# Attention kernel: the general path asked for behind each engine's own part, and more key tiles added on GpSimd in the last unit

## What is computed

```python
def _L0_gnn_ref(x, mask, Wq, bq, Wk, bk, Wv, bv, Wo, bo):   # 16 heads of 32
    q = heads(x @ Wq + bq); k = heads(x @ Wk + bk); v = heads(x @ Wv + bv)
    scores = jnp.einsum('bhqd,bhkd->bhqk', q, k) * scale
    scores = jnp.where(mask[:, None] == 0, -jnp.inf, scores)
    attn = jax.nn.softmax(scores, axis=-1)
    out = jnp.einsum('bhqk,bhkd->bhqd', attn, v)
    out = out.transpose(0, 2, 1, 3).reshape(b, s, D_MODEL)
    return out @ Wo + bo
h = jnp.maximum(_layernorm(x, axis=-1), 0.0)
x = x + _L0_gnn_ref(h, adj, Wq, bq, Wk, bk, Wv, bv, Wo, bo)
```

## Time and profile before

| | before |
|---|---|
| median of 3 runs (lowest to highest) | 1936.64 us (1936.35 to 1942.9) |
| the profiled execution, its own time | 1935.79 us |
| its span | 1933.9 us |
| mean granted clock of TensorE | 0.996 |
| PE busy | 1854.5 us (96%) |
| DVE busy | 1534.0 us (79%) |
| ACT busy | 1473.5 us (76%) |
| POOL busy | 1588.5 us (82%) |

### The profile page before, as it was taken

How to read it: one execution, slowest core, us unless ns; L and a number is a source line. 1 busy time by engine, 2 the same in 40 slices (tenths; PEclk the granted TensorE clock), 3 DMA queues, 4 the chain that set the end, 5 groups by cost and what they waited for, 6 DMA issues and landing times.

```text
span 1933.9 us, 35135 instructions
## 1 busy us (share of the span) xinstructions
PE 1854.5 (96%) x13856; PEld 767.9 (40%) x13856; DVE 1534.0 (79%) x1585; ACT 1473.5 (76%) x1772; POOL 1588.5 (82%) x701
## 2 busy tenths in 40 slices
PE   6989999999999999999999999999999999999997
PEld 4334434444344443444433443334344344343432
DVE  6788877887778887788877887778877788777775
ACT  4878886788867988678876788768887688867763
POOL 0988888887987979878889788888889889898873
PEclk9999999999999999999999999999999999999999
DMA  7532363523615335143442335423444224443121
GB/s 236 141 79 75 97 155 88 138 69 98 167 55 142 88 107 156 50 126 93 134 123 75 101 109 133 117 86 88 113 128 131 82 77 120 137 115 97 35 55 45
DMA packets 114136, 206.09 MB, mean 107 GB/s; under 512 B 12848, under 2 KB 16048, under 8 KB 113968
## 3 DMA queue, kind: packets, MB, share of 16 engines
q1 hardware_dynamic: 113104, 203.47, 38.1%
q10 hardware_dynamic: 864, 0.34, 0.1%
HBM read 153.43 MB, written 50.33 MB: 105 GB/s over the span
## 4 chain that ended last, share of the span: by engine, by line
PE 80%; DVE 10%; DMA 4%; ACT 3%; issue 2%; POOL 0%; SPq 0%; DVEq 0%; POOLq 0%; ACTq 0%
PE ps L783 21%; PE ps L770 20%; PE ps L738 14%; PE ps L820 8%; DVE ring L1068 8%; PE ps L752 7%; PE ps L745 7%; DMA k_stack<-k_parts 2%; ACT ring L905 1%; DMA k_parts<-k_part 1%; PE ps L734 1%; PE ps L793 1%; DVE oT_lo L1125 1%; ACT mask L966 1%; DMA ring<-x 0%
## 5 line engine op out<-in xcount | busy, mean ns | idle before, releaser
L1068 DVE TENSOR_TENSOR ring<-ps,mask 128x1024 f32<-128x1024 f32 x1024 | 1217.3, 1217 | 333.2 <-PE ps L770 306.5
L905 ACT ACTIVATE ring<-ring 128x1024 f32<-128x1024 f32 x1024 | 1062.4, 1050 | 236.1 <-DVE ring L1068 225.6
L1285 POOL TENSOR_TENSOR acc<-acc,ring 128x1024 f32<-128x1024 f32 x380 | 902.8, 2403 | 0.4 <-ACT ring L905 0.4
L1285 POOL TENSOR_TENSOR acc<-ring 128x1024 f32<-128x1024 f32 x252 | 608.8, 2427 | 305.0 <-ACT ring L905 300.4
L770 PE MATMUL ps<-q_stack,k_stack 128*128 128x512 f16 x2048 | 608.0, 382 | 49.3 <-DVE ring L1068 38.9
L783 PE MATMUL ps<-ring,v_sb 128*32 128x512 f32 x4096 | 505.9, 600 | 0.0
L770 PEld LDWEIGHTS ps<-q_stack,k_stack 128*128 128x128 f16 x2048 | 157.6, 97 | 415.9 <-DVE ring L1068 232.5
L783 PEld LDWEIGHTS ps<-ring,v_sb 128*32 128x32 f32 x4096 | 107.2, 109 | 263.2 <-issue 232.9
L820 PE MATMUL ps<-acc,ones 128*32 128x512 f32 x1008 | 131.3, 593 | 0.5 <-POOL acc L1285 0.5
L933 ACT ACTIVATE rden<-ps 128x512 f32<-128x512 f32 x64 | 38.3, 598 | 114.1 <-PE ps L820 114.1
L745 PE MATMUL ps<-wv_lo,hT_hi 128*128 128x128 f16 x1024 | 100.3, 219 | 0.0
(11 more groups left out here) (88 smaller groups left out, 1565.4 us busy)
## 6 DMA issues: line engine op xcount, KB each, us to landing
x_in<-x SPq DMA_DIRECT2D x172, 256.0 KB, 2.9
edges<-adjT SPq DMA_DIRECT2D x128, 256.0 KB, 3.8
q_stack<-q_parts SPq DMA_DIRECT2D x124, 256.0 KB, 4.8
k_stack<-k_parts SPq DMA_DIRECT2D x124, 256.0 KB, 4.8
q_parts<-q_part SPq DMA_DIRECT2D x64, 256.0 KB, 2.0
k_parts<-k_part SPq DMA_DIRECT2D x64, 256.0 KB, 2.1
out<-x_in SPq DMA_DIRECT2D x60, 256.0 KB, 2.0
ring<-x SPq DMA_DIRECT2D x4, 512.0 KB, 5.4
```

What stands on the lines that cost most here:

```text
L905: nc.scalar.activation(tile, tile, ACT.Exp, scale=SCALE / UP / UP).then_inc(s["prob_ready"], 1)
L1068: nc.vector.tensor_tensor(ring[:, slot_of(kt, pair), :].rearrange("p (a n) -> p a n", n=HALF), ps_s(j), mask[:, kt:kt + 1, half * HALF:(ha ...
L1285: nc.gpsimd.tensor_tensor(acc[:, group, pair, :], first_of, ring[:, slot_of(kt, pair), :], ALU.add).then_inc(s["sum_done"], 1)
```

## The change

Both paths now stand in one block: the general part of each engine follows directly on its main part, without the meeting in between, and a wait on the semaphore of the verdict stands before the load of the flag. SP's wait for the last stores comes behind its branch (`landed`). In the last unit, GpSimd makes part B in the first sweep as in all other units (key tiles 5 and 6), and in the last sweep it adds key tile 5 to 4 (`LAST_TERMS = "A67B"`). Two bias additions of the last unit move to the unit before it, and one small reduction of VectorE (L1187) moves from graph 5 to graph 7. `LAST_RECIPROCAL_AT` and `LAST_SCALE_O_AT` have the same values as before, so they move nothing.

```diff
-LAST_BIAS_AT = {(1, 24): 4, (1, 25): 5, (3, 8): 6, (3, 9): 7, (3, 14): 0, (3, 15): 1, (3, 24): 2, (3, 25): 3}
-LAST_TERMS = "A4567"
-UNIT_BLOCKS = {6: ("p0", "p1"), 10: ("p2", "p3"), 14: ("p4", "p5", "dA", "d4", "d5"), 18: ("p6", "d6", "p7", "d7")}
-LAST_BLOCKS = {6: ("p0", "p1"), 10: ("p2", "p3"), 14: ("p4", "p5", "dA", "d4", "d5"), 16: ("p6", "d6"), 17: ("p7", "d7")}
+LAST_BIAS_AT = {(1, 24): 4, (1, 25): 5, (2, 14): 6, (2, 15): 7, (3, 14): 0, (3, 15): 1, (3, 24): 2, (3, 25): 3}
+LAST_TERMS = "A67B"
+LAST_SUMS_AT = 8
+LAST_BLOCKS = {6: ("p0", "p1"), 10: ("p2", "p3"), 14: ("p4", "p5", "dA"), 16: ("p6", "d6"), 17: ("p7", "d7", "dB")}
...
 def terms_of(V):
-    return LAST_TERMS if V >= LAST_SWEEP - 1 else TERMS
+    return LAST_TERMS if V == LAST_SWEEP else TERMS
 def blocks_of(V):
-    return BLOCKS if V < LAST_SWEEP - 1 else UNIT_BLOCKS if V < LAST_SWEEP else LAST_BLOCKS
+    return BLOCKS if V < LAST_SWEEP else LAST_BLOCKS
...
-                    pe.wait_ge(s["sum_done"], sums_before(V) + SUMMED_AT[term])
+                    pe.wait_ge(s["sum_done"], sums_before(V) + (LAST_SUMS_AT if V == LAST_SWEEP and term == "B" else SUMMED_AT[term]))
...
-                        if last and up == UNITS - 1 and j % SWEEP // PAIRS >= 4:
+                        if last and up == UNITS - 1 and j >= SWEEP + 12:
                             continue
...
         def gated(eng, program):
+            eng.wait_ge(verdict_taken, 4)
             wanted = eng.value_load(flag, min_val=0, max_val=1)
             with eng.If(wanted > 0):
                 program()
...
             gated(sp, program)
+            landed(sp)
...
-            for k in range(X_SLOTS):
-                sp.wait_ge(stored[k], 16 * B * QT // X_SLOTS)
...
+        def landed(sp):
+            for k in range(X_SLOTS):
+                sp.wait_ge(stored[k], 16 * B * QT // X_SLOTS)
+        return landed, s["verdict_step"]
...
-    with nc.sbuf_tensor("flag", [1, 1], I32) as flag:
-        fast_attention(nc, x, adjT, Wq, bq, Wk, bk, Wv, bv_cols, Wo, bo, ident, headones, out, parts, flag)
-        general_attention(nc, flag[0:1, 0:1], x, adj, Wq, bq, Wk, bk, Wv, bv, Wo, bo, ident, out, scratch)
+    with ExitStack() as outer:
+        flag = outer.enter_context(nc.sbuf_tensor("flag", [1, 1], I32))
+        block = outer.enter_context(nc.Block())
+        landed, verdict_taken = fast_attention(nc, outer, block, x, adjT, Wq, bq, Wk, bk, Wv, bv_cols, Wo, bo, ident, headones, out, parts, flag)
+        general_attention(nc, block, landed, verdict_taken, flag[0:1, 0:1], x, adj, Wq, bq, Wk, bk, Wv, bv, Wo, bo, ident, out, scratch)
```

More of the change, by code:

```diff
@@ L18, with general_attention @@
 AX = mybir.AxisListType
-def general_attention(nc, flag, x, adj, Wq, bq, Wk, bk, Wv, bv, Wo, bo, ident, out, scratch):
+def general_attention(nc, block, landed, verdict_taken, flag, x, adj, Wq, bq, Wk, bk, Wv, bv, Wo, bo, ident, out, scratch):
     qT_s, kT_s, v_s, o_s = scratch
@@ L93, in general_attention @@
         qk_t = [s.rearrange("b (c p) (t n) -> b t p c n", p=P, n=P) for s in (qT_s, kT_s)]
-        block = ctx.enter_context(nc.Block())
         def gated(eng, program):
+            eng.wait_ge(verdict_taken, 4)
             wanted = eng.value_load(flag, min_val=0, max_val=1)
@@ L144, in program @@
             def program():
+                dve.wait_ge(loaded, WEIGHTS)
                 nc.vector.memset(eps[:], EPS).then_inc(eps_set, 1)
-                dve.wait_ge(loaded, WEIGHTS)
                 with dve.Fori(0, TOKT) as i:
@@ L329 @@
 MASK_AT = {3: [17, 18, 20, 22, 23, 25, 27, 29], 0: [1, 4, 5, 7, 11, 12, 14, 15]}
+RECIPROCAL_AT, SCALE_O_AT = 2, 5
+O_HIGH_AT, O_LOW_AT = [5, 15, 6, 5], [7, 19, 13, 7]
 MASK_FIRST = [2 * i - 3 for i in range(2, 2 * QT)]
 LIMIT_AT = 23
-RECIPROCAL_AT, SCALE_O_AT = 2, 5
-O_HIGH_AT, O_LOW_AT = [5, 15, 6, 5], [7, 19, 13, 7]
+LAST_RECIPROCAL_AT, LAST_SCALE_O_AT = 2, 5
 EDGE_SLOTS = 4
@@ L364, in sums_before @@
 def sums_before(V):
-    return SUMS * min(V, LAST_SWEEP - 1) + SUMMED_AT["A"] * max(0, V - LAST_SWEEP + 1)
+    return SUMS * V
 def spread_out(chunk, slots):
@@ L437, in two_before, with fast_attention @@
     return SEQUENCE[i - 2] if i >= 2 else None
-def fast_attention(nc, x, adjT, Wq, bq, Wk, bk, Wv, bv, Wo, bo, ident, headones, out, parts, flag):
+def fast_attention(nc, outer, block, x, adjT, Wq, bq, Wk, bk, Wv, bv, Wo, bo, ident, headones, out, parts, flag):
     ctx = ExitStack()
@@ L446, in sem @@
         def sem(name):
-            return ctx.enter_context(nc.semaphore(name))
+            return outer.enter_context(nc.semaphore(name))
         w_hi = [sb(f"w{n}_hi", [P, DC, D], F16) for n in "qkvo"]
@@ L977, in graph @@
                             weights_high(3)
-                        if j == RECIPROCAL_AT and not (first and up == 0):
+                        if j == (LAST_RECIPROCAL_AT if last and up == UNITS - 1 else RECIPROCAL_AT) and not (first and up == 0):
                             reciprocal(U * SWEEPS - 1)
-                        if j == SWEEP + RECIPROCAL_AT:
+                        if j == SWEEP + (LAST_RECIPROCAL_AT if last and up == UNITS - 1 else RECIPROCAL_AT):
                             reciprocal(U * SWEEPS)
-                        if last and up == UNITS - 1 and j == SWEEP + SCALE_O_AT + 1:
+                        if last and up == UNITS - 1 and j == SWEEP + LAST_SCALE_O_AT + 1:
                             o_high_last(0)
@@ L1176, in graph @@
                             weights_low(3)
-                        if j == SCALE_O_AT and not (first and up == 0):
+                        if j == (LAST_SCALE_O_AT if last and up == UNITS - 1 else SCALE_O_AT) and not (first and up == 0):
                             scale_o(U - 1, 1)
-                        if j == SWEEP + SCALE_O_AT:
+                        if j == SWEEP + (LAST_SCALE_O_AT if last and up == UNITS - 1 else SCALE_O_AT):
                             scale_o(U, 0)
@@ L1185, in graph @@
                             nc.vector.tensor_reduce(limits[:, LIM_W + n:LIM_W + n + 1], w_hi[n][:], AX.XY, ALU.max, apply_absolute_value=True)                                .then_inc(s["limits_ready"], 1)
-                        if up == 0 and b == 5 and j == LIMIT_AT:
+                        if up == 0 and b == B - 1 and j == LIMIT_AT:
                             nc.vector.tensor_reduce(limits[:, LIM_B:LIM_B + 1], b_up[:, 2, :], AX.X, ALU.max, apply_absolute_value=True)                                .then_inc(s["limits_ready"], 1)
                         if last and up == UNITS - 1:
-                            if j == SWEEP + SCALE_O_AT + 3:
+                            if j == SWEEP + LAST_SCALE_O_AT + 3:
                                 o_low_last(0)
```

## The result

The changed kernel takes 1941.76 us in the median of 22 runs, the kernel before 1935.49 in 22 runs beside them. The ratio is 1.0036 (95% interval 1.0027 to 1.0046): 5 to 9 us slower, about 7. Forecast were 1941.0 us and +4.4.

What follows compares the result with a forecast made beforehand. TensorE was taken to bound the kernel (80% of the chain), with an end of no busy engine; -5.45 - 0.86 + 11.1 + 2.0 - 1.9 - 0.5 = +4.4 us gave 1941.0 us, range 1934.0 to 1947.0.

Steps and rivals of the forecast that it cites:

- The end: Program end: TensorE's flag load and branch hide behind matmuls and stores, the last store's landing is late next; -5.45 us.
- One term less in the last sweep: TensorE in the last sweep: terms 4 and 5 go, B comes, without a wait; -0.86 us.
- The bracket: GpSimd, first sweep of the last unit: reduction with idle time around it takes 13.1 us, delaying key tile 6's additions.
- The shift of TensorE: Tile 18 of the last unit: TensorE stands at term B until GpSimd's sums are done, delaying later scores; +11.1 us.
- the clock: After TensorE's idle time in the last unit, B, p7 and d7 begin at 1.2 GHz; +2.0 us, bounds 0 and +2.6.
- VectorE's small steps: Last unit: two small VectorE operations no longer held by GpSimd's additions, -1.9 us; a 512-column one, -0.5.
- The moved pieces: Bias additions moved to the unit before and VectorE's moved small reduction: nothing for both.
- its low bound: Whole forecast with all unknown costs at their low ends, the earlier slow stretch gone too (-1.4): -0.8 us, 1935.8.
- Rival (a): Last unit: the wait for GpSimd isn't there, wholly or partly; total about -2.7 (1934.0) or -8.0 (1928.6); chance 0.12.
- Rival (b): Program end gives less: TensorE loads the flag late (-3.5) or SP pays for its branch (-2.35); 1943.0 or 1944.1; chance 0.18.
- Rival (c): Last unit: TensorE's clock stays low through short bursts, over 6 us at half clock, so slower; chance 0.08.

Runs made afterwards that it cites:

- experiment 1: Kernel before with only the one block for both paths added, sums, terms and bias additions as before; ratio 0.9984 to the kernel before.
- Experiments 6 and 7: On the kernel of experiment 3, TensorE, respectively SP, waits for the last stores before loading the flag; one run each, 1932.08 and 1940.59 us.
- experiment 3: Changed kernel, but key tile 5 is added on GpSimd only in the very last sweep, first sweep as before; ratio 0.9998 to the kernel before.
- experiment 5: Changed kernel with a small memset in place of GpSimd's reduction over partitions; single run 1927.56 us, the kernel before 1931.72 beside it.
- Experiment 2: Kernel before with only the added key tiles on GpSimd, two blocks kept; ratio 1.0040 to the kernel before.
- experiment 7: On the kernel of experiment 3, SP waits for the last stores before loading the flag; one run, 1940.59 us.
- experiment 8: Changed kernel, but the reduction is GpSimd's very last work and VectorE's three last verdict steps follow its last product step; 1925.39 us, ratio 0.9960 to the kernel before.

## Why the prediction was right, point by point

The mechanism and the sign came out as forecast: a wait of TensorE at term B that outweighs a shorter end. The size is near, in part because errors of its terms cancel. By its steps:

1. *The end:* forecast -5.45, measured -3.4 and -3.3 (changed kernel, experiment 1). TensorE's branch is hidden, as said; mis-sized was the landing, taken as the 2.0 us of before. The step said "the landing is late next, and it was there before too", and missed that what was hidden behind the stores, TensorE's fetch, slows them: the last store took 4.2 us to land, not 2.2. Experiments 6 and 7 show it. The Trainium skill's Runtime: NRT & Kernel Launch, Instruction fetch mechanics, says that an engine's sequencer fetches pages through a DMA queue of its own and that a taken branch out of the pages at hand waits for such a DMA; the trace agrees (a packet of 16 KB, a branch of 3.6 us). I had used the rule for the branch's duration alone, not for what it does to the others' transfers.
2. *One term less in the last sweep,* -0.86: in the changed kernel the last terms ran without a wait. It isn't separated by the runs: the ratio of experiment 3 resolves nothing so small.
3. *The bracket,* 13.1: it was 13.6, and less than 0.1 without the reduction (experiment 5).
4. *The shift of TensorE,* +11.1, and 5. *the clock,* +2.0: together 13.1, measured +13.9 at tile 20. The bracket gave 0.5 of the difference. The clock cost nearly its upper bound: B, p7 and d7 took 4.9 us, where 2.6 is full speed.
6. *VectorE's small steps:* the -1.9 came as forecast, 0.31 us for what took 2.32. L1133 took 2.36 instead of 2.82: -0.5, as forecast.
7. *The moved pieces:* no wait that would be theirs is in the trace.

From tile 20 to the last addition the changed kernel took 4.8 us less; steps 2 and 6 give 3.3 of it. The rest, 1.5, I put down to the stretch at half clock of the earlier trace rows, which cost 1.0 us on one block of matmuls and wasn't there after; the prediction had it at -1.4 in its low bound. No run tests it, but two traces bear it out. Experiment 1 has the orders of before and no such stretch, and took 36.5 us from tile 20 to the last addition, against 39.2 before; VectorE's three operations of the earlier trace rows account for 1.2 of that, which leaves 1.5. Against it the changed kernel (34.4) gained 2.1, and that is the term (0.86) and those three operations (3.93 us down to 2.67). Experiment 2, with the changed kernel's times for the three and one stretch of 3.4 us at half clock, took 36.05.

Added up, the trace is off the forecast by +2.1 at the end, +0.8 in steps 4 and 5 and -1.5 behind tile 20: +5.7 instead of +4.4. That the sum is nearer than its largest error is luck. The runs say +7 (5 to 9), so +4.4 itself lies just below their interval.

Rival (a) falls: the whole bracket stood in the way. Rival (b) was right in its outcome, an end that is only 3.4 us shorter, and wrong in both its causes: TensorE's queue loaded the flag early, and SP's branch took 50 ns. Rival (c), a low clock through the last unit, wasn't this result, but something near it happened in one execution of experiment 7.

The wider question, where the gain of the change went, has the answer of experiments 5 and 8: the sums and the block together are worth about 10 us against the trace of before (6.5 in the unit, 3.5 to 3.7 at the end), and one instruction that was left at its old place takes them away and 6 us more. Of the 6.5, 2.7 are what the unit of experiment 1 was faster with the orders of before, so by that trace the sums are worth 3.8; the runs of experiment 8 say 5 to 11 for both together.

## What to carry to other kernels

When work is moved to an engine with slack, read that engine's whole row of work, not its busy share: the rare instruction among it (here a reduction of 0.44 us that has nearly 6 us before it and 7 behind in which GpSimd does nothing else) belongs behind everything that someone waits for, or where nothing follows at all. What is hidden behind a transfer must not itself be a transfer: a branch's fetch of instructions is one.

## What the runs showed that I had not expected

- A fetch of instructions can hold up a store: with one 16 KB fetch and one or two of 8 KB beside it, the last 256 KB store landed in 3.9 to 4.3 us in the seven traces in which TensorE asks early, and in 2.2 in the three in which its branch comes behind the landing.
- A VectorE operation that takes 0.75 us while GpSimd stands still took 8.78 us once beside GpSimd additions that ran back to back, and 1.6 to 2.8 us in the nine other traces, all at the same place. In those nine it ended 0.55 us behind the first end of an addition that came after its start, with the next one running; in the one it let four such ends pass and ended 0.55 us behind the last. What decides how long it is held wasn't tried.
- At its branch TensorE pays 3.4 to 4.3 us, the other three engines 0.05 to 0.07, in every trace here, whether it comes while matmuls still run or behind the stores. Why TensorE's alone is long no run shows.
